# Eight weighted ranges instead of six in layer 2 of a fused GNN kernel, with layer 0's schedule rearranged

## What is computed

```python
x = layernorm(x + segment_sum(w * x[src], dst) ... )         # layer 0: edges read as row = src, col = dst; weighted
x = layernorm(x + gcn_twice_with_batchnorm(x))               # layer 1: two unweighted passes, 128 and 64 wide
x = layernorm(x + mlp((1 + eps) * x + segment_sum(w * x[src], dst)))  # layer 2: weighted, 256 wide
x = layernorm(x + relu(layernorm(gcn(x))))                   # layer 3: unweighted, 256 wide
```

## Time and profile before

| what | us |
|---|---|
| median of 3 runs (3420.88 to 3424.51) | 3422.25 |
| profiled execution, device time | 3420.75 |
| its span, first to last instruction | 3419.5 |
| PE busy | 2834.1 (83%) |
| POOL busy | 2469.3 (72%) |
| DVE busy | 1978.5 (58%) |
| ACT busy | 1165.9 (34%) |

### The profile page before, as it was taken

How to read it: one execution, slowest core, us unless ns; L and a number is a source line. 1 busy time by engine, 2 the same in 40 slices (tenths; PEclk the granted TensorE clock), 3 DMA queues, 4 the chain that set the end, 5 groups by cost and what they waited for, 6 DMA issues and landing times. The chain is left out here.

```text
span 3419.5 us, 60203 instructions
## 1 busy us (share of the span) xinstructions
PE 2834.1 (83%) x19220; PEld 2096.7 (61%) x19220; DVE 1978.5 (58%) x6483; ACT 1165.9 (34%) x3693; POOL 2469.3 (72%) x2238
## 2 busy tenths in 40 slices
PE   5999888879898869799968987678888875799995
PEld 3877666657776657344447774366666664466664
DVE  7899988877787546342253434433444564245557
ACT  5565565667776648000010003400111232001123
POOL 3888888887777665677747777777777775777773
PEclk9999999999999979899969997588999997799997
DMA  7787888889888888788837886755565554978884
GB/s 274 114 142 112 152 159 157 157 167 188 183 184 182 170 234 296 192 223 235 235 99 202 226 222 177 230 153 156 168 181 173 166 171 140 292 237 247 251 251 140
DMA packets 658435, 652.78 MB, mean 191 GB/s; under 512 B 87902, under 2 KB 606476, under 8 KB 656588
## 3 DMA queue, kind: packets, MB, share of 16 engines
q0 software_dynamic: 153600, 258.41, 37.5%
q1 hardware_dynamic: 430670, 331.83, 31.5%
q10 hardware_dynamic: 73854, 58.70, 5.5%
HBM read 434.19 MB, written 214.52 MB: 190 GB/s over the span
## 5 line engine op out<-in xcount | busy, mean ns | idle before, releaser
L1706 POOL DMA_INDIRECT A<-rows_buf,big x572 | 913.3, 1597 | 285.1 <-issue 148.6
L886 POOL DMA_INDIRECT rows_buf<-T,idx x888 | 851.2, 959 | 275.9 <-issue 272.5
L980 PE MATMUL PSA<-S,rows_buf 128*128 128x128 bf16 (+2 forms) x5904 | 586.3, 254 | 213.1 <-DMA rows_buf<-X,idx 97.3
L980 PEld LDWEIGHTS PSA<-S,rows_buf 128*128 128x128 bf16 (+2 forms) x5904 | 526.5, 143 | 294.6 <-DMA rows_buf<-X,idx 82.9
L886 POOL DMA_INDIRECT rows_buf<-X,idx x528 | 507.6, 961 | 160.9 <-issue 158.1
L1036 DVE TENSOR_TENSOR accT<-PSA,accT 128x256 f32 (+2 forms) x354 | 132.8, 375 | 833.4 <-PE PSA L980 831.0
L1387 PE MATMUL PSA<-XRS,rows_buf 128*128 128x256 f32 x1144 | 311.7, 397 | 3.8 <-DMA XRS<-in_xpad 3.8
L1553 DVE TENSOR_TENSOR accT<-PSA,accT 128x392 f32 (+5 forms) x366 | 239.7, 655 | 101.1 <-PE PSA L1484 45.9
L797 ACT ACTIVATE accT<-accT,vec 128x500 f32<-128x500 f32 (+3 forms) x26 | 17.7, 694 | 669.4 <-DVE accT L795 669.3
L1399 ACT ACTIVATE rows_buf<-PSA 128x512 f32<-128x512 f32 x286 | 168.7, 593 | 213.9 <-PE PSA L1387 204.0
L1387 PEld LDWEIGHTS PSA<-XRS,rows_buf 128*128 128x128 f32 x1144 | 209.8, 197 | 30.0 <-issue 5.1
(11 more groups left out here) (318 smaller groups left out, 5644.9 us busy)
## 6 DMA issues: line engine op xcount, KB each, us to landing
XRS<-Ad SPq DMA_DIRECT2D x400, 256.0 KB
Ad<-accT SPq DMA_DIRECT2D x224, 196.0 KB
XRS<-in_xpad SPq DMA_DIRECT2D x192, 128.0 KB, 4.1
Awd<-accT SPq DMA_DIRECT2D x48, 392.0 KB, 3.6
A<-accT SPq DMA_DIRECT2D x9, 1600.0 KB
rows_buf<-T,idx POOLq DMA_INDIRECT x888
rows_buf<-A SPq DMA_DIRECT2D x24, 512.0 KB
accT<-A SPq DMA_DIRECT2D x24, 512.0 KB, 7.3
```

The lines of the kernel that those rows point to most:

```text
L886: s_hg[slot(i)][j // 2].on(pool.indirect_dma_start(Gv(slot(i), j), None, table, bass.IndirectOffsetOnAxis(idx[:, c:c + 1], 0)), 16)
L980: last = pe.matmul(PS[bank_of(i)][0:F, W * h:W * h + W], Gv(slot(i), j)[:, o:o + F], hits[:, i % SRING, j, :], start=j + part == 0, stop=j ...
L1706: s_k[n].on(pool.indirect_dma_start(A, bass.IndirectOffsetOnAxis(tgt[:, c:c + 1], 0), G[:, i % RING, j, :], None, compute_op=ALU.add), 16)
```

## The change

Range matrices with weights are now made for eight ranges (`HWIN` = 8), and layer 2 takes them in two sets of four: 512 columns in a matmul, five gather slots, larger piece buffers. Layer 2 then gathers from group 73 on, not 63: 122 groups, not 132. In layer 0 the planner's result changes with `HWIN`: 386 units, `DENSE0` = 107, and the 49 dense blocks fall into the 34 steps 107 to 140, two of them in 15 steps and one in 19. The second block of such a step is turned and multiplied directly behind the first one's product. The 16 first chunks use two copies of A, and the third is zeroed by SP during steps 0 to 4, from one smaller zeroed area that ACT writes first. `unit_places_known` runs after step 1 and `unit_keys` inside step 2. DVE's wait for the zeroing moves from the first unit to the first use of buffer 1. Chunks 252 to 291 are units of one chunk and 10 slots (490 columns) with weights; before they were units of two chunks and 20 slots (980 columns) without.

```diff
-HWIN = 6
+HWIN = 8
+TWOCOPIES = 16
-CLASSES = ((0, 64, 4, 8), (64, 120, 2, 8), (120, 160, 2, 10), (160, HOTW, 1, 8),
+CLASSES = ((0, 64, 4, 8), (64, 120, 2, 8), (120, 160, 2, 10), (160, 252, 1, 8), (252, HOTW, 1, 10),
            (HOTW, 376, 2, MAXN), (376, 448, 1, 14), (448, HOT, 1, 16))
+def copy_of(c):
+    early = 0 <= c - BND[XWIN] < TWOCOPIES
+    return c % 2 if early else c % COPIES
 def taken(k, i):
-    return sum(c % COPIES == k for c in range(CG * G0, CG * (G0 + i + 1)))
+    return sum(copy_of(c) == k for c in range(CG * G0, CG * (G0 + i + 1)))
...
-    for b in range(4):
-        s_q.on(sc.activation(zeros[:, 3200 * b:3200 * b + 3200], ...))
+    blank = zeros[:, 3136:6272]
+    for lo, hi in ((3136, 6272), (0, 3136), (6272, 9408), (9408, 2 * AW)):
+        s_q.on(sc.activation(zeros[:, lo:hi], ...))
...
+    def zero_part(k, b):
+        s_q.by(sp, 1)
+        if b < 4:
+            to = A[AR * k:AR * k + 6272, :].rearrange("(p r) d -> p (r d)", p=128)
+            s_zero[k].on(sp.dma_start(to[:, 3136 * b:3136 * b + 3136], blank), 16)
+        else:
+            s_zero[k].on(sp.dma_start(A[AR * k + 6272:AR * k + AR, :], blank[0:AR - 6272, 0:D]), 16)
...
-            if u.at == 0:
+            if u.first and buffer_of(u.w) == 1 and user_before(u.w) is None:
                 for s in s_zero:
                     s.by(v)
-            else:
+            if u.at:
                 v.wait_ge(s_ae, u.turns[half])
...
-        for k in range(1, COPIES):
-            zero_copy(k)
+        zero_copy(1)
...
             for t in blocks:
+                if t != blocks[0]:
+                    dense_turn(t)
+                    dense_turned(t)
+                    if t + 2 < NT:
+                        dense_load(sc, t + 2)
                 dense_product(t)
                 dense_out(t)
...
-            for t in range(NT):
-                if dense_step(t) == i:
+            for t in [t for t in range(NT) if dense_step(t) == i][0:1]:
...
             transfers(i + 2)
+            if i < 5:
+                zero_part(2, i)
...
+            if i == 2:
+                unit_keys()
             for u in following[0:1]:
                 onehots(u)
...
-            if i == 0:
+            if i == 1:
                 unit_places_known()
-            if i == 1:
-                unit_keys()
...
-    G2 = rb[:, 0:6 * CG * D].rearrange("p (r j n) -> p r j n", r=6, j=CG)
+    G2 = rb[:, 0:5 * CG * D].rearrange("p (r j n) -> p r j n", r=5, j=CG)
...
-           ..., [rb[:, 6144:6912], rb[:, 6912:7680], weights[:, 768:1536]], Awd, per=3, split=1, slots=6, step=2,
+           ..., [rb[:, 5120:6144], rb[:, 6144:7168], weights[:, 768:1792]], Awd, per=4, split=1, slots=5, step=2,
```

More of the change, by code:

```diff
@@ L289, in build @@
     quadw = lambda ap: ap.bitcast(BF16).rearrange("p (w j) -> p w j", j=CG)
-    SuH = quadw(early[:, 12208:12464])
+    SuH = quadw(early[:, 12256:12512])
     curD = early[:, 6776:7560].rearrange("p (g c) -> p g c", c=CG)
@@ L397, in build @@
     zeros = accT[:, :, :].rearrange("p h n -> p (h n)")
-    for b in range(4):
-        s_q.on(sc.activation(zeros[:, 3200 * b:3200 * b + 3200], nought[:, 0:1].broadcast_to([128, 3200]), ACT.Identity))
+    blank = zeros[:, 3136:6272]
+    for lo, hi in ((3136, 6272), (0, 3136), (6272, 9408), (9408, 2 * AW)):
+        s_q.on(sc.activation(zeros[:, lo:hi], nought[:, 0:1].broadcast_to([128, hi - lo]), ACT.Identity))
     s_io.on(pool.iota(iti, pattern=[[1, W]], base=0, channel_multiplier=0))
@@ L514, in scatter_rows @@
             n = len(range(k, NG * CG, COPIES))
-            v.tensor_scalar(srcAv[:, bass.ds(k, n, COPIES)], srcv[:, bass.ds(k, n, COPIES)], float(AR * k), None, ALU.add)
+            last = v.tensor_scalar(srcAv[:, bass.ds(k, n, COPIES)], srcv[:, bass.ds(k, n, COPIES)], float(AR * k), None, ALU.add)
+        link(last)
+        first, n = BND[XWIN], TWOCOPIES // 2
+        for k in range(2):
+            v.tensor_scalar(srcAv[:, bass.ds(first + k, n, 2)], srcv[:, bass.ds(first + k, n, 2)], float(AR * k), None, ALU.add)
         link(v.tensor_scalar(spare[:, :, :], srcf[:, :, :], -1.0, pidx[:, 0:1], ALU.mult, ALU.add))
@@ L1213, in build @@
     x2T = accT[0:64, 1, 0:N]
-    def zero_copy(k):
[L1217 to L1222, removed]
+    def zero_part(k, b):
[5 more added lines that the diff above has]
+            s_zero[k].on(sp.dma_start(A[AR * k + 6272:AR * k + AR, :], blank[0:AR - 6272, 0:D]), 16)
+    def zero_copy(k):
+        for b in range(5):
+            zero_part(k, b)
     def load_weights():
@@ L1699, in spread @@
                     pool.wait_ge(s_yc, 2 * i + j // 2 + 1)
-                n = c % COPIES
+                n = copy_of(c)
                 if uses[n]:
@@ L2314, in build @@
     hybrid(X2, D, wide, HWIN, 2, lambda part, h, b: X2s[:, b, 128 * h:128 * h + 128], lambda: load_table(X2, X2s),
-           lambda slot, j: G2[:, slot, j, :], [rb[:, 6144:6912], rb[:, 6912:7680], weights[:, 768:1536]], Awd, per=3, split=1, slots=6, step=2,
+           lambda slot, j: G2[:, slot, j, :], [rb[:, 5120:6144], rb[:, 6144:7168], weights[:, 768:1792]], Awd, per=4, split=1, slots=5, step=2,
            weighted=True, paced=PACE2, steps=second_tail, pairs=1, hot=hot4,
```

## The result

The changed kernel takes 3453.26 us (median of 4 runs, 3448.16 to 3455.56); the kernel before took 3421.57 us beside it (3419.76 to 3424.51). The ratio is 1.0093, 95% interval [1.0077, 1.0109]: 31.8 us slower. The forecast was 3412 us in a range that ended at 3444; both its sign and its range are wrong. The profiled execution spans 3446.9 us, 27.4 us more than before's 3419.5.

The account below looks back on a forecast made before the run. POOL was taken to nearly set layer 0's pace until the dense blocks, then something else, and to bound layer 2's pass. Terms -46 - 6 + 6 - 7 + 43 = -10 us gave 3411, stated as 3412 us, range 3378 to 3444.

Parts of the forecast that it names:

- Layer 2's pass, -46: Layer 2's gather pass: 10 groups fewer at 5.06 us, -50.6 us, plus 4 us for a stall.
- The stall of 4 us: Layer 2's pass near group 108: POOL stalls with five slots; 4 us added, bounded by 0 and 25.
- PE bounds layer 2's pass: Rival, layer 2's pass: PE at 94% adds 0.3 us for each of 90 groups, 27 us, giving 3439; chance 0.12.
- Start, -6: Layer 0's start: scatters begin earlier with two copies, but PE gains only some 5 us; -6 us, ends -18 and 0.
- the rival built on it: Rival, layer 0's start: DVE's moved setup blocks keep scatters back, 4.7 us more, giving 3417; chance 0.08.
- Dense doubles, +43: Layer 0, two dense blocks in 15 of 34 steps: 3.4 us each, +51, less 8 absorbed by store waits.
- the term for the two more weighted ranges, +6 us: Layer 0: added DVE and PE work mostly fits in idle time under POOL's floor; +6 us, ends 0 and +25.
- the -7 of steps 92 to 106: Layer 0, steps 92 to 106 without dense blocks: 15 x (8.28 - 7.83), -7 us, ends -12 and 0.
- only moves: Layer 0, first dense load: its wait of 8.4 us moves with the dense blocks and adds nothing.
- Stores hold the second block: Rival, layer 0's double steps: late dense stores delay the second block's eviction, 41 us more, giving 3453; chance 0.20.
- Hidden second block: Rival, layer 0's double steps: the second block hides behind other work, dense term +5, giving 3374; chance 0.14.

Follow-up runs that it names:

- thin_dve: Changed kernel with VectorE's weight products and weighted evictions of ranges 6 and 7 cut to 1 row and 1 block: ratio 1.0069 to the kernel before.
- thin_mended: Changed kernel, dense loads first, second block turned early, dense stores by ScalarE, VectorE's weight work of ranges 6 and 7 cut to a sliver: 0.9982 of the kernel before.
- loads_first: Changed kernel with SyncE issuing the first dense loads ahead of range 15's table store: ratio 1.0085 to the kernel before.
- after_old_setup: Changed kernel with the old setup order (three copies zeroed first, both setup blocks at steps 0 and 1): ratio 1.0110 to the kernel before.
- dense_alone: Kernel before, six ranges kept, with only the dense blocks moved to start at step 107, two in 15 steps: ratio 1.0054 to the kernel before.
- no_second: Changed kernel with 14 second dense blocks loaded and stored but not turned, multiplied or copied out: ratio 1.0069 to the kernel before.
- thin_pe: Changed kernel with two of the three weighted matmuls per unit of ranges 6 and 7 left out: ratio 1.0105 to the kernel before.

## Why the prediction was wrong, step by step

**Layer 2's pass, -46: right.** -51.7 in the table, -42.8 [-50.3, -35.6] alone. The stall of 4 us was not there, and the rival *PE bounds layer 2's pass* fell with it.

**Start, -6: right in size, wrong in its reason.** I named PE as what holds the early steps. The trace names the landing of the scatter two before, on two copies. With six ranges the gain lasts (4.4 us); with eight it doesn't. The moved setup blocks ran on DVE from 35.3 to 53.2 us and met three scatters (37.04, 44.94 and 50.16), not eight. These last 1.90, 1.65 and 1.54 us, 0.5 us together over three times the minimum of 1.53, and the first scatter took 1.90 in the kernel before as well. The Trainium skill, page "SBUF — State Buffer", section "Who interferes with whom", would have a two-port DVE instruction shut GpSimd out for its length; which of these instructions are of that kind the trace doesn't say, but no scatter was held up for more than 0.4 us, and the rival built on it fell.

**Dense doubles, +43: near in size, in part by luck.** +48.5 us in the stretch, the chain as forecast, and some 4 us for a double where I had 3.4. But 14 doubles taken out gave back only 24.8 us, and 39.1 with the stores and the first loads moved too; 9.4 us are there with a single double left. Of DVE's added work some 15 us lie in these steps (122.5 + 88.2 us busy before, 129.3 + 96.9 after); whether that is the 9.4 wasn't tried. Alone, with 13 to 17 us of lead at its start, the same doubles cost +27.3. I had counted on PE being the pace either way, which holds only without lead.

**The step that failed** is the term for the two more weighted ranges, +6 us, with its words "the lighter steps between pay it back". Together with the -7 of steps 92 to 106 it said -1 us for steps 3 to 106; they came out at +39.3. Three things are in it, with 12.2, 10.6 and 16.5 us:

1. *DVE had less room than I gave it.* In steps 77 to 106 DVE's busy time rises from 87.6 + 99.9 to 104.8 + 105.3 us, by 22.6. Steps 77 to 105 grow from 232.6 to 244.8 us, although those from 92 on no longer have dense blocks. The forecast added 39 us to DVE and let the idle time of other steps take it. That idle time wasn't free: thin_dve took 27.3 us off DVE and brought steps 77 to 105 down to 227.8 us, and with thin_mended 15 of 15.7 us came back in steps 77 to 106.
2. *The cover of the first load.* I wrote that the wait of 8.4 us "only moves". It moved from step 92, before which the messages were 11 to 14 us ahead, to step 106, where they were 1.0 ahead, and became 12.7 us on POOL. Step 106 takes 19.8 us for 9.2 before; loads_first took 6.9 of these off.
3. *Steps 3 to 76*, +16.5 us, with DVE's busy time unchanged (513.0 and 510.4 us, x1321 and x1322). The idle time grew. All ten traces with eight ranges and the new setup have it: 589.2 to 593.7 us there, against 571.2 to 578.2 in the five with six. DVE's waits in this stretch, before and then after (L1553 and L1580 of before are L1570 and L1597 of after):

```profile
DVE accT L1553 <- ACT accT L1569: 6.9, 2, 3.5
...
DVE accT L1580 <- DMA Awd<-accT: 2.4, 2, 1.8
```
```profile
DVE accT L1597 <- DMA Awd<-accT: 10.9, 7, 2.7
DVE accT L1570 <- ACT accT L1586: 7.7, 3, 3.1
```

More of the tables is stored in it (80 parts of counts for 70, 40 of weights for 39), and DVE's waits for stores and clears grew from 9.3 to 18.6 us. PE stands behind DVE there; its waits for DVE's count evictions, before and then after:

```profile
PE PSA L1496 <- DVE accT L1553: 46.3, 44, 6.2
```
```profile
PE PSA L1513 <- DVE accT L1570: 61.1, 46, 9.4
```

That is 14.8 us more. The mean granted clock is lower too, 0.96 for 0.98; with eight ranges it goes from 0.96 with 593.7 us (after) to 0.97 with 588.2 (after_old_setup), so some of the 16.5 us may be the clock's, but 588.2 is still 11 us over before. How the three share the 16.5 us stays open, and no run changed the turnover alone.

The -7 us of steps 92 to 106 was right for what it described: dense_alone has -6.6 there.

**The rivals.** *Stores hold the second block* came nearest in time (3453 us), but not by its mechanism: in steps 107 to 124 ScalarE waited for no store, and in after all such waits are 20.7 us, fewer than before's 31.0. Such waits do stand behind the doubles (no_second, 42.9 us). *Hidden second block* is wrong without lead and half right with it. No rival described the doubles and the late load as costs that a bank of 14 us had paid; the range ended 9 us short for that.

**What stays open**: the 60 us between the parts and the whole are placed by stretch (against each part alone, about 22 in steps 3 to 91, 25 in 92 to 106, over 20 in 107 to 141, each read from single traces), but the first has only waits that grew with it, no run that took them out.

## What to carry to other kernels

Where two engines are joined by a ring, read from the trace how far the producer is ahead at each stage, and treat it as an account: an idle share, or a wait of the producer that "costs nothing", is worth only what the account holds at that place. A change that lightens one pass by loading another has to be priced at the place where the account is empty, and parts that look cheap alone (-4.4, -42.8, +18.5 us) then don't tell what the whole costs (+31.8); price or build the last part, here the two ranges, by itself as well. When a test takes work off an engine, look whether the engine's busy time fell by that much: in thin_pe it fell by 5.0 us of 17, with a lower granted clock beside it.

## What the runs showed of the hardware

The landing of a scatter took 10 us in the first steps, beside the stores that zero the third copy, and at most three starts of 1.85 us, 5.5 us, in the run with three copies; that the zero stores make the difference was not tried. Four table stores on one queue that wait for each other take 7.7 to 11.8 us (910.63 to 918.32 in the fence above), and everything that SyncE issues behind them is late by that: the first dense blocks were issued 11 us after what they needed was free.
